# A graph layer and a mixture of experts: token groups of 7 x 512, 256, 128 and 128, and a first expert octet beside the list

## The chip, the cores and the metric

The kernel runs on one core of a Trainium2 chip. The metric is the device time of one execution in microseconds; the time before is the median of three runs, 401.93 us (399.69 to 402.66).

## What is computed

Two layers, each added to its input. The first mixes the rows of all 4096 tokens by a dense 4096 x 4096 adjacency matrix; the second sends each token to two of 64 experts.

```python
def _L0_gnn_ref(x, adj, kernel, bias, beta):
    scale = jnp.reciprocal(jnp.sum(adj, axis=1) + beta)
    agg = adj @ x + beta[:, None] * x
    return scale[:, None] * agg @ kernel + bias

def _L0_ffn_ref(x, Wr, br, W1, b1, W2, b2):
    ...
    logits = xf @ Wr + br
    topk_logits, topk_idx = jax.lax.top_k(logits, TOP_K)       # TOP_K = 2
    gates = jax.nn.softmax(topk_logits, axis=1)
    ...
    for e in range(E):                                          # E = 64
        h = jax.nn.relu(xf @ W1[e] + b1[e])                     # 128 -> 256
        y = h @ W2[e] + b2[e]                                   # 256 -> 128
        out = out + combine[:, e:e + 1] * y
...
x = x + _L0_gnn_ref(_layernorm(x, axis=-1), adj, ...)
x = x + _L0_ffn_ref(_layernorm(x, axis=-1)[None], ...)[0]
```

## The kernel before

Work on each engine is written out by hand, in the order in which that engine runs it; semaphores tie the engines together. TensorE is PE in the profile, VectorE DVE, ScalarE ACT, GpSimd POOL, SyncE SP.

**Aggregation.** The 4096 tokens are 32 tiles of 128, taken in eight groups of four (512 tokens). For a group g, the adjacency columns come in eight chunks of 1 MB through a ring of five slots (`adj_ring`, loaded on SP's queue). A chunk holds four tiles of 128 source tokens by 512 columns. TensorE adds up z^T x chunk in the PSUM bank `agg_ps[g % 2]`. Most chunks are split into a high and a low part: ScalarE rounds the chunk (`round_chunk`, line 584), VectorE subtracts (`low_part`, line 716), and TensorE runs three fast products for each tile (lines 973, 974, 977). The others are whole chunks (`whole_chunk`, line 963): one 32-bit product a tile. Seven chunks of each group from the second on are split (51 in all), and the last, which holds the group's own rows, is whole, since VectorE first adds beta on its diagonal (`add_diag`).

**The steps of a group.** While TensorE aggregates group g, the steps of group g - 1 run between its products at fixed tile numbers (`step`): `copy_agg` (ACT), `gnn` (PE, the weight product and the degree), `residual` with statistics (DVE), `root` (ACT), `shifts` (DVE), `normalise` (ACT, writes z1), `turn_z1` (PE), `copy_z1t` (ACT), `router` (PE), `choose` (DVE, the two experts of each token), `ranks` (PE, each token's place among its expert's), `place` (DVE), and `dispatch` (POOL), which scatters each token's row to its expert's rows in memory, eight indirect DMAs a group. For the last group these steps stand alone.

**Two lists of expert tiles.** An expert tile is 128 rows of one expert. The early list is made from the first seven groups: 16 full tiles, whose starts are known while the last group is still under way. The list of the remaining tiles needs all tokens: `total_done`, 26 small VectorE steps (lines 823 to 853), a transposition on TensorE, and the two tables `table` and `skip_tab`. TensorE runs 13 and 12 products of no effect (`warm`, line 918) around that transposition.

**Expert tiles.** Eight slots. Each tile needs its weights and rows (loaded on SP's queue for slots 0 to 3, on ACT's for 4 to 7), then `turn_x` (PE, line 1039), `copy_xt` (DVE, 874), `up` (PE, 1045), `relu` (DVE, 884), `down` (PE, 1052 and 1055), `copy_y` (ACT, 645) and an indirect scatter of the answers (POOL, 542). `ahead` runs the three PE steps and the two DVE steps with distances of up to three tiles. The number of tiles in groups of four, `quads`, is read from `table` into a register by every engine. SP and ACT load the tiles of the next octet as slots come free. At the end both answers of a token are read back and summed with the gates.

## Time and profile before

| | |
|---|---|
| median of the runs | 401.93 us (399.69 to 402.66) |
| the profiled execution's own time | 402.74 us |
| its span | 400.9 us |
| TensorE busy | 345.6 us, 86% |
| VectorE busy | 306.9 us, 77% |
| ScalarE busy | 171.0 us, 43% |
| GpSimd busy | 224.7 us, 56% |
| mean granted clock of TensorE | 0.941 of full speed |

The span is the time from the first to the last instruction in the trace; the profiled execution took 1.84 us more. Busy time is that of the instructions themselves, an average over stages with different limits. A row of the timeline gives start and duration in us, engine, line of the program, operation, what it writes and reads, how many instructions are merged, and in brackets the idle time before and what ended it. For TensorE one row can hold several records; a 32-bit product makes two.

### The profile page before, as it was taken

How to read it: one execution, taken by the hardware profiler on the slowest of the kernel's cores; microseconds unless marked ns; L12 is line 12 of the kernel's file. 1: busy time of each engine (PE TensorE's matmuls, PEld its weight loads, DVE VectorE, ACT ScalarE, POOL GpSimd, SP SyncE). 2: the span in 40 equal slices, each digit the busy share in tenths (PEclk: the TensorE clock that was granted, in tenths of full speed). 3: DMA queues.
4: the chain of work that ended last, by engine and by line, in shares of the span. 5: the costliest groups of instructions: out<-in, count | busy, mean ns of one | idle time of the engine just before them, and what ended most of it. 6: DMA issues, size and time to landing. Idle time of an engine off the chain costs nothing.

```text
span 400.9 us, 8275 instructions
## 1 busy us (share of the span) xinstructions
PE 345.6 (86%) x1975; PEld 276.7 (69%) x1975; DVE 306.9 (77%) x907; ACT 171.0 (43%) x265; POOL 224.7 (56%) x220
## 2 busy tenths in 40 slices
PE   5999898997999999999999835999999999999100
PEld 2445684884886868868778522799999999999000
DVE  3769779779889899898998568676777776777067
ACT  2475665556665855748646031111222212122063
POOL 4450002038877847768578354657777777777500
PEclk9799999998999999999999966999999999999855
DMA  8999999995996978969965017499999999995097
GB/s 308 361 428 366 345 425 367 370 428 241 381 425 251 417 319 329 411 244 412 385 263 216 13 41 256 124 317 285 308 293 291 296 292 289 293 291 163 25 372 257
DMA packets 45624, 119.26 MB, mean 298 GB/s; under 512 B 7705, under 2 KB 19630, under 8 KB 37410
## 3 DMA queue, kind: packets, MB, share of 16 engines
q1 hardware_dynamic: 27938, 95.88, 63.7%
q10 hardware_dynamic: 12672, 14.58, 11.9%
q0 software_dynamic: 4992, 8.54, 5.8%
q8 instruction: 9, 0.15, 0.1%
q14 instruction: 13, 0.11, 0.1%
HBM read 104.02 MB, written 16.78 MB: 301 GB/s over the span
## 4 chain that ended last, share of the span: by engine, by line
PE 39%; DVE 33%; DMA 14%; ACT 7%; issue 4%; POOL 1%; SPq 0%; POOLq 0%; DVEq 0%; ACTq 0%
DVE adj_low L716 16%; DMA adj_ring<-adj_t 9%; PE bank L1045 9%; PE bank L963 8%; PE bank L1055 5%; PE bank_pair L1055 5%; ACT adj_high L584 4%; ACT payload L599 2%; PE bank L1039 2%; PE bank_pair L1052 2%; PE bank L1052 2%; DVE x_sb L905 2%; DVE adj_ring L745 2%; DVE top_i L755 2%; DMA expert_answers<-adj_ring,ans 2%
## 5 line engine op out<-in xcount | busy, mean ns | idle before, releaser
L716 DVE TENSOR_TENSOR adj_low<-adj_ring,adj_high 128x2048 fp32r<-128x2048 f32 x51 | 116.1, 2286 | 19.7 <-ACT adj_high L584 19.3
L584 ACT CAST adj_high<-adj_ring 128x2048 fp32r<-128x2048 f32 x51 | 97.1, 1905 | 60.0 <-DMA adj_ring<-adj_t 36.2
L529 POOL DMA_INDIRECT dispatched_rows<-payload,slot x64 | 94.4, 1475 | 46.2 <-DMA dispatched_rows<-pad_rows 19.3
L542 POOL DMA_INDIRECT expert_answers<-adj_ring,ans x92 | 90.4, 983 | 31.9 <-issue 18.6
L973 PE MATMUL bank<-adj_high,z_hi 128*128 128x512 f32 x204 | 84.4, 414 | 0.0
L974 PE MATMUL bank<-adj_high,z_lo 128*128 128x512 f32 x204 | 79.7, 391 | 0.0
L884 DVE TENSOR_SCALAR adj_ring<-bank,adj_ring 128x128 f32<-128x128 f32 x184 | 56.1, 346 | 8.8 <-PE bank L1045 6.2
L1045 PE MATMUL bank<-xt_sb,adj_ring 128*128 128x128 f32 x368 | 56.2, 275 | 0.3 <-DVE xt_sb L874 0.3
L977 PE MATMUL bank<-adj_low,z_hi 128*128 128x512 f32 x204 | 54.8, 390 | 0.9 <-DVE adj_low L716 0.9
L963 PE MATMUL bank<-adj_ring,z_sb 128*128 128x512 f32 x104 | 51.3, 645 | 3.1 <-DVE z_sb L702 3.1
L1045 PEld LDWEIGHTS bank<-xt_sb,adj_ring 128*128 128x128 f32 x368 | 48.4, 192 | 0.5 <-DVE xt_sb L874 0.5
L518 POOL TENSOR_TENSOR more<-mask 128x128 bf16<-128x128 bf16 x8 | 12.9, 1618 | 59.2 <-DVE mask L761 59.1
L977 PEld LDWEIGHTS bank<-adj_low,z_hi 128*128 128x128 f32 x204 | 38.2, 188 | 9.6 <-DVE adj_low L716 1.3
L973 PEld LDWEIGHTS bank<-adj_high,z_hi 128*128 128x128 f32 x204 | 38.4, 188 | 9.0 <-issue 1.8
L974 PEld LDWEIGHTS bank<-adj_high,z_lo 128*128 128x128 f32 x204 | 38.4, 188 | 8.8 <-issue 1.7
L963 PEld LDWEIGHTS bank<-adj_ring,z_sb 128*128 128x128 f32 x104 | 20.9, 208 | 27.0 <-issue 25.7
L645 ACT COPY adj_ring<-bank_pair 128x128 f32<-128x128 f32 x46 | 11.3, 267 | 63.5 <-PE bank_pair L1055 58.3
L879 DVE TENSOR_TENSOR ans<-adj_ring,skip_tab 128x1 int32<-128x1 f32 x92 | 14.9, 162 | 22.5 <-DMA expert_answers<-adj_ring,ans 20.4
L1055 PE MATMUL bank_pair<-adj_ring 128*128 128x128 f32 x184 | 28.7, 278 | 0.1
L1055 PE MATMUL bank<-adj_ring 128*128 128x128 f32 x184 | 28.6, 278 | 0.1
L645 ACT COPY adj_ring<-bank 128x128 f32<-128x128 f32 x46 | 12.1, 267 | 37.7 <-PE bank L1055 34.7
L874 DVE COPY xt_sb<-bank 128x128 f32<-128x128 f32 x92 | 25.7, 281 | 1.8 <-PE bank L1039 1.8
(151 smaller groups left out, 424.6 us busy)
## 6 DMA issues: line engine op xcount, KB each, us to landing
adj_ring<-adj_t SPq DMA_DIRECT2D x64, 1024.0 KB, 9.2
adj_ring<-w_pack SPq DMA_DIRECT2D x48, 257.5 KB
adj_ring<-w_pack ACTq DMA_DIRECT2D x44, 257.5 KB
dispatched_rows<-pad_rows SPq DMA_DIRECT2D x8, 528.0 KB, 12.0
adj_ring<-expert_answers SPq DMA_DIRECT2D x8, 512.0 KB, 6.6
adj_ring<-dispatched_rows SPq DMA_DIRECT2D x48, 66.0 KB
adj_ring<-dispatched_rows ACTq DMA_DIRECT2D x44, 66.0 KB
out<-x_sb SPq DMA_DIRECT2D x8, 256.0 KB, 4.2
```

Of the source, the lines that this page charges most:

```text
L529: pool.indirect_dma_start(rows, bass.IndirectOffsetOnAxis(ap=slot[:, b, t, k:k + 1], axis=0), payload[:, b, t, k, :], None).then_inc(scatt ...
L542: pool.indirect_dma_start(y_tok, bass.IndirectOffsetOnAxis(ap=ans[:, s:s + 1], axis=0), y_sb[:, s, :], None, bounds_check=N * K - 1, oob_i ...
L584: nc.scalar.copy(high[:, m % PARTS], adj_sb[:, slot_of(g, k)]).then_inc(hi_ready, 1)
L716: v.tensor_tensor(low[:, m % PARTS], adj_sb[:, slot_of(g, k)], high[:, m % PARTS].bitcast(F32), ALU.subtract).then_inc(lo_ready, 1)
L874: v.tensor_copy(xt_sb[:, s % 2, :], xt_ps[s % 2][:, 0:P]).then_inc(xt_ready, 1)
L884: last = v.tensor_scalar(h_sb[:, s % DEEP, c, :], up_ps[s % 2][:, c * P:(c + 1) * P], w_sb[:, s, B1_COL + c:B1_COL + c + 1], 0.0, ALU.add, ...
L963: last = mm(agg_ps[g % 2][:], z_sb[:, j, :], adj_sb[:, slot_of(g, k), u, :], start=(k + u == 0), stop=(k + 1 == CHUNKS and u + 1 == CJ))
L973: mm(agg_ps[g % 2][:], z_hi[:, first + u, :], high[:, m % PARTS, u, :], start=(k + u == 0), stop=False)
L974: mm(agg_ps[g % 2][:], z_lo[:, first + u, :], high[:, m % PARTS, u, :], start=False, stop=False)
L977: last = mm(agg_ps[g % 2][:], z_hi[:, first + u, :], low[:, m % PARTS, u, :], start=False, stop=False)
L1045: last = mm(up_ps[s % 2][:, c * P:(c + 1) * P], w_sb[:, s, c * P:(c + 1) * P], xt_sb[:, s % 2, :], start=True, stop=True)
L1055: last = mm(y, h_sb[:, s % DEEP, c, :], w_sb[:, s, H + c * D:H + (c + 1) * D], start=False, stop=(c == HC - 1))
```

## The change

It cuts the last 512 tokens into groups of 256, 128 and 128. `TILES_OF` gives the tiles of each group, `FULL` (7) is the group of 256. A chunk stays 1 MB: it holds eight source tiles of 256 columns, or sixteen of 128, so the groups have 4, 2 and 2 chunks. Of these only three chunks of the group of 256 are split. The steps of the small groups stand at tile numbers of their own. The early list is still made from the first seven groups, now during the group of 128 that comes next. All eight early loads are on SP's queue, and they wait until the chunks but the last two are used. The first eight expert tiles are written out ahead of the loop and no longer wait for the list; VectorE's steps for the list stand between them, in five parts. The warming products around the list are gone. The ring starts one slot further on, and a few PSUM banks are used otherwise (`last_ps` is the logits' bank, so the fourth tile's answer goes to the first bank).

```diff
-GROUPS = N // GN
+TILES_OF = (4, 4, 4, 4, 4, 4, 4, 2, 1, 1)
+GROUPS = len(TILES_OF)
+FIRST_TILE = tuple(sum(TILES_OF[:g]) for g in range(GROUPS))
+FULL = TILES_OF.index(2)
...
-SPLIT = 7
 FIRST_SPLITS = (5, 6)
+SPLITS = tuple((g, k) for g in range(GROUPS)
+               for k in (FIRST_SPLITS if g == 0 else range(7) if g < FULL else range(3) if g == FULL else ()))
...
+        def ahead_once(turn, s, steps):
+            for distance, step in steps:
+                n = s + distance
+                step(turn + n // SLOTS, n % SLOTS)
...
             sp.wait_ge(early_table_ready, 1)
-            starts = load_starts(SP, early_table, 0, SP_SLOTS)
-            for s in range(SP_SLOTS):
+            starts = load_starts(SP, early_table, 0, SLOTS)
+            sp.wait_ge(chunk_used, chunk_no(GROUPS - 1, 0))
+            for s in range(SLOTS):
                 load_weights(sp, starts[s], s)
-            wait_scattered_before_last(sp)
-            for s in range(SP_SLOTS):
+            wait_full_scattered(sp)
+            for s in range(SLOTS):
                 load_rows(sp, starts[s], s)
...
+            for g in range(FULL, GROUPS):
+                if g == GROUPS - 2:
+                    act.wait_ge(early_list_turned, 1)
+                    nc.scalar.copy(early_table[:], early_ps[0:1, E:E + EARLY]).then_inc(early_table_ready, 1)
+                copy_agg(g)
+                root(g)
+                normalise(g)
+                copy_z1t(g)
...
+            residual(FULL)
+            shifts(FULL)
+            add_diag(FULL + 1)
+            list_early()
+            choose(FULL)
+            for g in range(FULL + 1, GROUPS):
+                residual(g)
+                if g + 1 < GROUPS:
+                    add_diag(g + 1)
+                    place(g - 1)
+                    shifts(g)
+                else:
+                    shifts(g)
+                    place(g - 1)
+                choose(g)
             place(GROUPS - 1)
...
-            for half in range(2):
-                ahead(dve, 0, half, None, steps)
+            for s in range(SLOTS):
+                ahead_once(0, s, steps)
+                if s == 0:
+                    list_counts()
+                if s == 1:
+                    list_totals()
+                if s == 2:
+                    list_experts()
+                if s == 3:
+                    list_starts()
+                if s == 5:
+                    list_to_tables()
+                if s == 6:
+                    make_gates()
+            dve.wait_ge(skip_ready, 1)
+            dve.wait_ge(table_ready, 1)
+            quads = quads_in_use(dve)
...
+            def step_last(j):
+                if j == 2:
+                    gnn(FULL + 1)
+                if j == 5:
+                    ranks(FULL)
+                if j == 14:
+                    turn_z1(FULL + 1)
+                if j == 17:
+                    router(FULL + 1)
+                if j == 24:
+                    ranks(FULL + 1)
...
-            warm(13, turn_ps)
-            pe.wait_ge(list_ready, 1)
-            nc.tensor.transpose(last_ps[0:2, 0:P], lst[:], ident[:])
...
-            warm(12, turn_ps)
...
+            pe.wait_ge(seen_ready, GROUPS)
+            mm(last_ps[:, 0:E], ones_b[:], seen[:], start=True, stop=True).then_inc(total_done, 1)
+            steps = [(3, turn_x), (0, down), (2, up)]
+            for s in range(SLOTS):
+                if s == SLOTS - 1:
+                    pe.wait_ge(skip_ready, 1)
+                ahead_once(0, s, steps)
+                if s == 4:
+                    pe.wait_ge(list_ready, 1)
+                    nc.tensor.transpose(last_ps[0:2, 0:P], lst[:], ident[:])
+                    mm(last_ps[:, P:2 * P], ones_f[:], again_diag[:], start=True, stop=True).then_inc(list_turned, 1)
+            pe.wait_ge(table_ready, 1)
+            quads = quads_in_use(pe)
+            with pe.Fori(1, OCTETS) as turn:
```

TensorE's queue from the end of the aggregation to the first expert tile, before (L963 is the aggregation, L930 `gnn`, L1039 `turn_x`):

```order
L963 MATMUL bank<-adj_ring,z_sb 128x512 x4
L1013 MATMUL bank<-seen,ones_b 128x64 [waits seen_ready]
L930 MATMUL bank_pair<-gnn_w_and_degree,agg_sb 128x129 [waits agg_copied,wd_ready,var1]
L930 MATMUL bank_pair<-gnn_w_and_degree,agg_sb 128x129 x3
L936 MATMUL bank<-ident,payload 128x128 [waits z1_ready]
...
L1022 MATMUL bank_pair<-seen,ones_b 128x64 [waits seen_ready]
L918 MATMUL bank<-ones_b 128x512 x13
L1025 MATMUL bank_pair<-ident,lst 2x128 [waits list_ready]
L1026 MATMUL bank_pair<-again_diag,ones_f 128x128
L918 MATMUL bank<-ones_b 128x512 x12
L333 TENSOR_LOAD table [waits table_ready,skip_ready]
L333 ISA x2
L1039 MATMUL bank<-ident,adj_ring 128x128 [waits xt_ready,tile_in0]
```

The same place after (L1064 is the aggregation, L1027 `gnn`, L1033 `turn_z1`, L1039 `router`, L1048 and L1049 `ranks`, L1180 `turn_x`):

```order
L1064 MATMUL bank<-adj_ring,z_sb 128x128 x8
L1027 MATMUL bank_pair<-gnn_w_and_degree,agg_sb 128x129 [waits agg_copied,wd_ready,var1]
L1033 MATMUL bank<-ident,payload 128x128 [waits z1_ready]
L1039 MATMUL bank<-wr_sb,z1t 128x64 [waits z1t_ready]
L1048 MATMUL bank<-mask,before 128x64 [waits seen_ready,mask_ready]
L1049 MATMUL bank<-seen,ones_b 128x64
L1180 MATMUL bank<-ident,adj_ring 128x128 [waits xt_ready,tile_in0]
L1180 MATMUL bank<-ident,adj_ring 128x128 [waits xt_ready,tile_in1]
L1186 MATMUL bank<-xt_sb,adj_ring 128x128 [waits h_ready,xt_ready]
```

The list's products and the warming ones have left this place, and each step has one tile in place of four. The same engine within the last group of 128, after (L1051 is the end of `ranks` of the group of 256):

```order
L1027 MATMUL bank_pair<-gnn_w_and_degree,agg_sb 128x129 [waits agg_copied,wd_ready,var1]
L1064 MATMUL bank<-adj_ring,z_sb 128x128 x3
L1048 MATMUL bank<-mask,before 128x128 [waits seen_ready,mask_ready]
L1049 MATMUL bank<-seen,ones_b 128x128
L1051 MATMUL bank<-mask,ones_b 128x64
L1064 MATMUL bank<-adj_ring,z_sb 128x128 x9
L1033 MATMUL bank<-ident,payload 128x128 [waits z1_ready]
L1064 MATMUL bank<-adj_ring,z_sb 128x128 x2
L1064 MATMUL bank<-adj_ring,z_sb 128x128 [waits diag_added,adj_in4]
L1039 MATMUL bank<-wr_sb,z1t 128x64 [waits z1t_ready]
L1064 MATMUL bank<-adj_ring,z_sb 128x128 x7
```

Steps that had 32 tiles of 512 columns around them stand between tiles of 128 here. VectorE's queue at the first expert tiles, before (L853 and L856 end the list, L874 is `copy_xt`, L879 and L884 `relu`):

```order
L853 TENSOR_SCALAR again_diag<-ident,again 128x128 [waits dve_own]
L856 CAST table<-bank_pair 2x128 [waits dve_own,list_turned]
L858 TENSOR_SCALAR skip_tab<-bank_pair,iota_back 128x128
...
L333 TENSOR_LOAD table [waits dve_own,skip_ready]
L333 ISA x2
L874 COPY xt_sb<-bank 128x128 [waits up_done,x_turned] x2
L879 TENSOR_TENSOR ans<-adj_ring,skip_tab 128x1
L884 TENSOR_SCALAR adj_ring<-bank,adj_ring 128x128 [waits down_done,up_done]
L884 TENSOR_SCALAR adj_ring<-bank,adj_ring 128x128
L874 COPY xt_sb<-bank 128x128 [waits up_done,x_turned]
```

And after (L896 follows the last `place`, L956 `copy_xt`, L961 and L966 `relu`, L900 the list's first step):

```order
L896 TENSOR_TENSOR diff<-top 128x32
L956 COPY xt_sb<-bank 128x128 [waits up_done,x_turned] x2
L961 TENSOR_TENSOR ans<-adj_ring,skip_tab 128x1
L966 TENSOR_SCALAR adj_ring<-bank,adj_ring 128x128 [waits down_done,up_done]
L966 TENSOR_SCALAR adj_ring<-bank,adj_ring 128x128
L956 COPY xt_sb<-bank 128x128 [waits up_done,x_turned]
L961 TENSOR_TENSOR ans<-adj_ring,skip_tab 128x1
L966 TENSOR_SCALAR adj_ring<-bank,adj_ring 128x128 [waits down_done,up_done]
L966 TENSOR_SCALAR adj_ring<-bank,adj_ring 128x128
L956 COPY xt_sb<-bank 128x128 [waits up_done,x_turned]
L900 TENSOR_SCALAR spare<-bank 128x64 [waits total_done]
```

The whole list has moved from ahead of the first `copy_xt` to behind the fourth, and its parts stand behind one tile each.

## Rows read from the trace of the kernel before

**Rows 1.** Stretches: PE, PEld, DVE, ACT, POOL busy (instructions), then PEclk, DMA share, GB/s.
```profile
202.50:228.40 25.90, 25.57 (x118) 19.40 (x117) 21.13 (x44) 10.78 (x12) 17.10 (x13) 1.00 0.46 184
228.40:253.70 25.30, 12.80 (x56) 7.24 (x57) 16.23 (x84) 5.21 (x10) 13.87 (x17) 0.73 0.42 140
270.70:378.60 107.90, 100.32 (x869) 98.22 (x869) 73.33 (x313) 20.39 (x80) 82.52 (x84) 0.99 0.86 262
```

**Rows 2.** Timeline of GpSimd: the ninth and the last of 92 answer scatters.
```profile
270.71 0.98 POOL L542 DMA_INDIRECT expert_answers<-adj_ring,ans  x1 [3.07 <-ACT adj_ring L645]
...
377.54 0.98 POOL L542 DMA_INDIRECT expert_answers<-adj_ring,ans  x1 [0.31 <-issue]
```

**Rows 3.** Timeline of ScalarE: the eighth tile's copy to the ninth's.
```profile
265.07 0.27 ACT L645 COPY adj_ring<-bank 128x128 f32<-128x128 f32 x1 [0.96 <-PE bank L1055]
...
265.75 1.21 ACTq L351 DMA_DIRECT2D adj_ring<-dispatched_rows  x1
269.58 0.43 ACT L645 COPY adj_ring<-bank_pair 128x128 f32<-128x128 f32 x2 [4.25 <-PE bank L1055]
```

**Rows 4.** Timeline of TensorE: chunks, the tail's transposition and router, the first tile.
```profile
94.10 5.20 PE L963 MATMUL bank<-adj_ring,z_sb 128*128 128x512 f32 x8
...
198.80 3.68 PE L963 MATMUL bank<-adj_ring,z_sb 128*128 128x512 f32 x8
...
206.06 0.40 PE L973 MATMUL bank<-adj_high,z_hi 128*128 128x512 f32 x1
...
208.79 0.39 PE L973 MATMUL bank<-adj_high,z_hi 128*128 128x512 f32 x1
...
224.68 3.68 PE L963 MATMUL bank<-adj_ring,z_sb 128*128 128x512 f32 x8
...
235.86 1.12 PE L936 MATMUL bank<-ident,payload 128*128 128x128 f32 x4 [5.60 <-ACT payload L599]
237.65 1.97 PE L942 MATMUL bank<-wr_sb,z1t 128*128 128x64 f32 x8 [0.68 <-ACT z1t L606]
...
253.67 0.38 PE L1039 MATMUL bank<-ident,adj_ring 128*128 128x128 f32 x2
```

**Rows 5.** Timeline of VectorE: two low parts, then the tail's residual and choice.
```profile
201.86 4.49 DVE L716 TENSOR_TENSOR adj_low<-adj_ring,adj_high 128x2048 fp32r<-128x2048 f32 x2
...
230.29 0.18 DVE L721 RECIPROCAL scale<-bank_pair 128x4 f32<-128x4 f32 x1 [3.74 <-PE bank_pair L930]
...
239.66 0.42 DVE L750 TENSOR_TENSOR logits<-bank,br_sb 128x256 f32<-128x256 f32 x1 [2.80 <-PE bank L942]
...
242.40 0.42 DVE L761 TENSOR_TENSOR mask<-hot 128x256 bf16<-128x256 f32 x1
```

**Rows 6.** Timeline of VectorE: first and last of 26 steps of the list.
```profile
245.56 0.22 DVE L823 TENSOR_SCALAR spare<-bank_pair 128x64 f32<-128x64 f32 x1
...
250.35 0.29 DVE L853 TENSOR_SCALAR again_diag<-ident,again 128x128 f32<-128x128 f32 x1
```

**Rows 7.** Timeline of VectorE: the ReLU of the first tile and of the second.
```profile
255.07 0.61 DVE L884 TENSOR_SCALAR adj_ring<-bank,adj_ring 128x128 f32<-128x128 f32 x2 [0.54 <-PE bank L1045]
...
255.86 0.60 DVE L884 TENSOR_SCALAR adj_ring<-bank,adj_ring 128x128 f32<-128x128 f32 x2
```

**Rows 8.** TensorE in the expert tiles: timeline, and the group of the weight loads.
```profile
256.29 0.61 PE L1045 MATMUL bank<-xt_sb,adj_ring 128*128 128x128 f32 x4
256.73 0.27 PE L1039 MATMUL bank<-ident,adj_ring 128*128 128x128 f32 x1
...
257.51 0.61 PE L1045 MATMUL bank<-xt_sb,adj_ring 128*128 128x128 f32 x4
...
L1045 PEld LDWEIGHTS bank<-xt_sb,adj_ring 128*128 128x128 f32 x368 | 48.4, 192 | 0.5 <-DVE xt_sb L874 0.5
```

**Rows 9.** Timeline of SyncE's queue: four early weight loads.
```profile
241.87 2.01 SPq L348 DMA_DIRECT2D adj_ring<-w_pack  x4
```

**Rows 10.** A stretch of the tail, columns as in rows 1.
```profile
234.00:247.00 13.00, 6.92 (x26) 4.14 (x27) 8.52 (x43) 3.41 (x7) 4.58 (x8) 0.50 0.36 123
```

More of the change, by code:

```diff
@@ L47 @@
 BUFS, DEEP = 2, 4
+LIST_BANK = 3
 EARLY = 2 * SLOTS
@@ L749, in choose @@
                 dve.wait_ge(logits_done, g + 1)
-                own.after(v.tensor_tensor(logits[:], logit_ps, br_sb[:, None, :].to_broadcast([P, GT, E]), ALU.add))
-                for t in range(GT):
-                    last = v.max(top[:, g * GT + t, :], logits[:, t, :])
+                span, count = span_of(g), TILES_OF[g]
+                own.after(v.tensor_tensor(logits[:, span], logit_ps[:, span], br_sb[:, None, :].to_broadcast([P, count, E]), ALU.add))
+                for n, t in enumerate(tiles_of(g), FIRST_TILE[g]):
+                    last = v.max(top[:, n, :], logits[:, t, :])
@@ new lines, in list_experts @@
+            def list_experts():
+                v.tensor_reduce(first, lw[:], AX_X, ALU.max)
+                v.scalar_tensor_tensor(out=own_handled[:], in0=iota_e[:], scalar=expert, in1=handled[:], op0=ALU.is_equal, op1=ALU.mult)
+                own.after(v.scalar_tensor_tensor(out=own_spare[:], in0=iota_e[:], scalar=expert, in1=spare[:], op0=ALU.is_equal, op1=ALU.mult))
+                v.tensor_reduce(latest, own_spare[:], AX_X, ALU.add)
+                own.after(v.tensor_reduce(held, own_handled[:], AX_X, ALU.add))
@@ L1005, in step @@
-                    if j == 20:
-                        router(g - 1)
-                    if j == 28:
-                        ranks(g - 1)
-                for k in range(CHUNKS):
+                    if g < FULL:
+                        step_full(g, j)
+                    elif g == FULL:
+                        step_half(j)
+                    elif g == FULL + 1:
+                        step_next(j)
+                    else:
+                        step_last(j)
+                for k in range(chunks_of(g)):
```

458 lines of the change are left out of this document (257 added, 201 removed).

## Prediction

> **What bounds the kernel now.** Read by stages, the span falls into a first part that is alike in both kernels up to about 202 us, the last group of 512 tokens (202.5 to 228.4), a tail (228.4 to 253.7), the expert tiles (to 378.6) and the final sum. Up to 228.4 VectorE sets the pace with the splits of the adjacency chunks: 21.1 of 25.9 us [rows 1]. In the tail nothing is full: TensorE works 12.8 of 25.3 us at a mean clock of 0.73, and one chain of small steps goes from engine to engine. The expert stage looks as if TensorE bounded it (100.3 of 107.9 us). GpSimd's own rows say otherwise [rows 2]: from the answer that starts at 270.71 to the last at 377.54 there are 83 steps of 1.287 us, without one break. So from the ninth tile on GpSimd's answer scatters are the bound, and **the end of the span is the start of the ninth scatter plus a constant**: 83 x 1.287 us and a last part that the change doesn't touch. What the change is worth is read at 270.71. That scatter waited 3.07 us for ScalarE's copy of 269.58 [rows 2, 3], and the copy was late because ScalarE, after the eighth tile's copy (265.07), issues loads and reads the list into registers: 4.5 us from one to the other.
>
> So the sum has four terms, each between marks of its own: (a) the end of the last aggregation product, now 228.4; (b) from there to the first transposition of an expert tile, now 253.67 [rows 4]; (c) from there to the eighth answer's copy, now 11.4 us later; (d) from there to the ninth scatter, 5.6 us.
>
> **(a) The last 512 tokens as groups of 256, 128 and 128: later by 10.0 us.** Four chunks fewer are split (47 in place of 51); that frees VectorE and ScalarE, but neither bounds this stretch any more. What bounds it is TensorE's order with three dependent chains in it.
>
> Group of 256: a split chunk's 12 products of 512 columns take 2.73 us (206.06 to 208.79) [rows 4], so 0.114 for one of 256 columns; I take 0.12. After the preceding whole chunk (198.80 with 3.68, so to 202.1 in steady order) 56 of them and 1.3 us for the preceding group's weight product bring TensorE to 210.2. There it waits for z1 of that group. VectorE ends its last low part at 206.35 and begins the residual; from the residual to the transposition of z1 takes 5.57 us in the tail (230.29 to 235.86) [rows 4, 5], where no split stands between, so 211.85. This wait of 1.6 us is new. Transposition, copy and router follow: 1.12 and 1.97 us in the rows, which were at half clock (0.50 from 234 to 247) [rows 10], so 0.6, 0.6 and 1.0, to 214.1. Ten more split products and six tiles of the whole chunk (8 records in 3.68 us for 512 columns, so 0.44 a tile) go to 218.1. The choice (239.66 to 242.82, 3.16 us) [rows 5] is there at 217.3, so the ranks don't wait. They and two tiles end the group at 219.4.
>
> Each group of 128 has 32 tiles of 128 columns. Their price stands in the expert stage, with 32-bit products of that very shape: 4 records from 256.29 to 256.73, 0.111 each [rows 8], two a tile, 7.1 us for 32. The first group has inside it the preceding one's steps (1.55 us), the early list's transposition (0.3) and 0.1 of waiting: 9.0 us, to 228.4. The second has 1.5 us of steps and waits about 0.75 for its z1, since the first one's residual, statistics and normalising (some 3.5 us) are longer than the tiles put before it: 9.35 us, to 237.8. With 0.6 for hand-overs that I don't see, 238.4. From both sides: no wait and no missed hand-over gives 236.5, a fall of the clock after the long wait and a late chain 241. I take 238.4, the sum of the rows.
>
> **(b) From the last product to the first tile: 25.3 us become 7.6.** What goes is three quarters of each step, the list of the remaining tiles (245.56 to 250.64 on VectorE, 5.1 us) [rows 6] with its transposition, and the warming products ahead of the tiles. What stays is a chain for one tile, estimated from the same steps for four: copy 0.27, product 0.4, residual and statistics 1.1, root 0.3, reciprocal and shift 0.35, normalising 0.6, transposition 0.3, copy 0.3, router 0.4, choice 1.25, ranks 0.3, place and difference 1.1: 6.7, and 0.9 for some fifteen hand-overs. The signal that lets TensorE begin a tile stands on VectorE behind that last place. The first tile starts at 238.4 + 7.6 = 246.0. Ends: 7.0 without hand-overs, 9.2 if the steps shrink less than that.
>
> Costed at nothing, with their cover: SyncE now issues all eight early loads, at 0.5 us an issue [rows 9]. The table is ready at about 228.4, some 2 us go for registers and 8 for sixteen issues, so the last is out at 238.5, 7 us ahead; without this cover the late tiles would cost their delay. ScalarE's wait for the early table stands ahead of the first small group's copy, but the transposition it waits for is ahead of that group's last product in TensorE's queue. GpSimd scatters the last two groups by about 249; behind them stand all answers, and the first is there at 251, so 2 us are the cover.
>
> **(c) The first eight tiles: 11.4 us become 15.6.** The list's steps now stand between the tiles on VectorE. A tile alone takes 0.79 us there (255.07 to 255.86) [rows 7], against 1.22 on TensorE (256.29 to 257.51) [rows 8]: the slack of eight tiles is 3.4 us. Into it go 5.1 us of list and 0.5 for the two steps of the tables, each like the list's last (0.29). VectorE therefore runs without a break: way in 2.2 us (253.67 to 255.86), six tiles 4.7, list 5.6, a ReLU 0.5, the last product 0.7, which is 13.7. To it comes the clock. At 94.10 a whole chunk took 5.20 us in place of 3.68 [rows 4]: half clock for twice the difference, 3 us, under steady products. Nothing warms TensorE between 238.4 and 246 in the changed kernel, so I let the first tiles run 3 us at half clock: 1.0 on the way in and 0.9 in the first tile. That makes 15.6 us, 261.6 for the eighth copy. Ends: 12.5 (list in the slack, clock up), 22 (all eight at half clock). TensorE's two new waits, for the list after the fifth tile and for the skip table before the eighth, have all later products queued behind them; VectorE is the late one there in any case, and its delay is already counted.
>
> **(d) The hand-over to the ninth tile: unchanged**, 5.6 us: ScalarE's instructions are the same and the table is ready by then. A row issue of 1.21 us [rows 3] may shrink to the usual third of it: 0 to -0.9. The ninth scatter then starts at 267.2 against 270.71.
>
> **Sum.** +10.0 - 17.7 + 4.2 + 0 = **-3.5 us**. On the profiled execution's 402.74 us that is 399.2; the runs' median, 401.93, is 0.8 lower, so **398.4 us**, 0.9% faster. 1% (4 us) is about what a measurement of this kernel can tell from no change.
>
> **A rule that speaks against it.** The 128-column records of the expert stage follow each other at 0.111 us, though the weight loads beside them last 0.192 us each [rows 8]: the loads overlap. The Trainium skill, TensorE: Matmul & The Clock Gate, section "LDWEIGHTS (loading the stationary operand)", gives a load the time of its columns, 107 ns for 128, and its section on weight-path modes says that the fast load isn't for FP32. Were such a load paid beside every record of the small groups, an estimate from that page is 128 x 0.107 = 13.7 us more. The rows of the expert stage don't agree with that.
>
> **Rivals.** *Loads not hidden (slower).* The products of the small groups go at the pace of their weight loads: 128 records x (0.192 - 0.111) = 10.4 us, and 72 split products of 256 columns x 0.07 = 5.0, so +15.4 - 3.5, or 413.8 us. It decides from a pitch of 0.14 us (no gain) and 0.17 (1% slower). For it: narrow products need a load four times as often. Against it: the 368 records of that shape in the expert stage. Chance 0.06.
>
> *The clock.* Each fall costs what it cost at 94.10, 1.5 us. The changed tail has two waits that could bring one (1.6 and 0.75 us), and the eight tiles may stay at half clock for longer. Two falls give 401.4 us, no change; with all eight tiles at half clock 404 to 407. For it: the warming products are gone. Against it: the two waits are shorter than the stretch from the tail's last step (231) to its fall. Chance 0.16, half of it slower by over 1%.
>
> *The list is hidden after all.* If VectorE's steps fit beside the tiles, (c) is 12.4 and the sum -6.7: 395.2 us. For it: the last tiles have slack again. Against it: 5.6 us don't go into 3.4. Chance 0.12.
>
> **How the numbers follow.** The forecast has 0.66, with a range of its own of 395 to 401.5 from the ends of (a) and (b); two fifths of that lie beyond 1% faster. So faster 0.27 + 0.12 and a little for an easier boundary, 0.41; slower 0.06 + 0.08, 0.14; within 1% 0.45. The range for 8 in 10 is 394.5 to 403.5: it takes in the hidden list and two falls of the clock, and leaves out the paid loads and eight tiles at half clock.
>
> **What would show it.** In the new profile the last 128-column aggregation product should end near 238, and records of that shape should follow at 0.11 us. The first tile's transposition should stand near 246, the eighth copy near 261.6, the ninth scatter near 267, and from there steps of 1.287 us with no break to the last; the span should be near 397.4. VectorE should have nearly no idle time in the first five tiles. I am wrong if GpSimd has breaks after the ninth answer, if the last aggregation product ends beyond 241, or if the clock is still half after 250.

## The result and the profile after

The changed kernel takes **396.46 us** (median of 18 runs, 393.78 to 399.89) against 400.49 us for the kernel before (18 runs, 399.03 to 402.66). The ratio is 0.9886, 95% interval 0.9865 to 0.9907: 1.1% faster, or 4.6 us with an interval of 3.7 to 5.4. The forecast was 3.5 us, 398.4 us from the 401.93 us of the first three runs (397.0 from the 400.49 of all 18), and "within 1%". The profiled execution took 396.82 us, its span is 395.0 us and its mean granted clock 0.954.

Read first by stages. The marks are those of the prediction's four terms: the start of the seventh group's last whole chunk and ScalarE's copy of the last aggregation product, then the first tile's transposition and the eighth copy, and last the end of the scatters. Columns as in [rows 1].

```profile
198.93:234.40 35.47, 33.33 (x265) 31.25 (x263) 23.04 (x92) 7.26 (x17) 23.90 (x28) 1.00 0.53 191
234.40:241.65 7.25, 1.51 (x8) 0.89 (x8) 4.11 (x21) 1.43 (x4) 2.36 (x4) 0.83 0.66 220
241.65:257.25 15.60, 14.49 (x101) 13.18 (x102) 13.10 (x69) 3.38 (x9) 7.92 (x9) 0.86 0.54 158
257.25:373.10 115.85, 105.48 (x917) 103.22 (x915) 77.43 (x334) 21.85 (x85) 84.47 (x86) 0.98 0.85 257
```

The tail of 25.3 us is 7.25 us long, the stage ahead of it is longer, and VectorE is busy for 13.10 of the 15.60 us of the first eight tiles. TensorE's timeline (start, duration, line, idle time before and what ended it) answers to [rows 4 and 8].

```profile
195.81 3.68 PE L1064 MATMUL bank<-adj_ring,z_sb 128*128 128x512 f32 x8
...
208.84 0.66 PE L1033 MATMUL bank<-ident,payload 128*128 128x128 f32 x4 [1.22 <-ACT payload L655]
...
218.00 3.38 PE L1064 MATMUL bank<-adj_ring,z_sb 128*128 128x128 f32 x28
...
229.60 0.33 PE L1033 MATMUL bank<-ident,payload 128*128 128x128 f32 x1 [0.60 <-ACT payload L655]
...
232.34 2.03 PE L1064 MATMUL bank<-adj_ring,z_sb 128*128 128x128 f32 x16
237.82 0.33 PE L1033 MATMUL bank<-ident,payload 128*128 128x128 f32 x1 [2.54 <-ACT payload L655]
...
241.65 0.66 PE L1180 MATMUL bank<-ident,adj_ring 128*128 128x128 f32 x2 [0.92 <-DVEq L950]
...
266.08 0.33 PE L1180 MATMUL bank<-ident,adj_ring 128*128 128x128 f32 x1 [0.25 <-DMA adj_ring<-dispatched_rows]
...
267.91 0.33 PE L1180 MATMUL bank<-ident,adj_ring 128*128 128x128 f32 x1 [0.39 <-DMA adj_ring<-dispatched_rows]
...
271.61 0.32 PE L1180 MATMUL bank<-ident,adj_ring 128*128 128x128 f32 x1 [2.26 <-DMA adj_ring<-dispatched_rows]
```

Three things are to be seen. The chunk that starts at 198.80 in [rows 4] starts at 195.81 here, though nothing ahead of it was to change. The two forecast waits for z1 are there (1.22 and 0.60 us). And three transpositions wait for rows from memory. TensorE transposes three tiles ahead of the one that it finishes, so these are the 18th to the 20th tile, the second to the fourth that SyncE loads for the third octet. (The expectations below call them tiles 14 to 16, by a miscount of mine.) ScalarE's timeline from the eighth copy to the ninth answers to [rows 3], GpSimd's (the ninth, the 17th, the 25th and the last answer) to [rows 2].

```profile
257.25 0.27 ACT L698 COPY adj_ring<-bank 128x128 f32<-128x128 f32 x1 [0.96 <-PE bank L1200]
...
257.93 0.34 ACTq L387 DMA_DIRECT2D adj_ring<-dispatched_rows  x1
260.59 0.43 ACT L698 COPY adj_ring<-bank_pair 128x128 f32<-128x128 f32 x2 [3.08 <-PE bank_pair L1200]
```
```profile
261.71 0.98 POOL L588 DMA_INDIRECT expert_answers<-adj_ring,ans  x1 [2.24 <-ACT adj_ring L698]
...
273.84 0.98 POOL L588 DMA_INDIRECT expert_answers<-adj_ring,ans  x1 [2.13 <-ACT adj_ring L698]
...
285.62 0.98 POOL L588 DMA_INDIRECT expert_answers<-adj_ring,ans  x1 [1.79 <-ACT adj_ring L698]
...
371.90 0.98 POOL L588 DMA_INDIRECT expert_answers<-adj_ring,ans  x1 [0.30 <-issue]
```

GpSimd now has two breaks behind the ninth answer, where the prediction had none. From ninth to last it takes 110.19 us in place of 106.83: 3.36 us are given back.

Because the profiled executions differ ahead of any change, each term is counted from the start W of that last whole chunk of the seventh group (198.80 before, 195.81 after). A second profile of the changed kernel was taken (W at 199.68).

| us | before | forecast | after | after, again |
|---|---|---|---|---|
| (a) W to the copy of the last aggregation product | 29.60 | 39.6 | 38.60 | 38.61 |
| (b) to the first tile's transposition | 25.27 | 7.6 | 7.24 | 7.25 |
| (c) to the eighth copy | 11.40 | 15.6 | 15.60 | 15.70 |
| (d) to the ninth scatter | 5.64 | 5.6 | 4.46 | 4.51 |
| W to the ninth scatter | 71.91 | 68.4 | 65.90 | 66.07 |
| ninth to last scatter | 106.83 | 106.83 | 110.19 | 107.34 |

### The profile page after: what moved, and what is told of

Its sections match the earlier page's. It is cut to its first block, busy times and chain, and to the rows that moved or that the text cites. A ratio compares the mean times of both kernels' runs of the same rounds, so it can differ in the third digit from the quotient of the medians.

```text
span 395.0 us, 8459 instructions
## 1 busy us (share of the span) xinstructions
PE 341.3 (86%) x2076; PEld 282.6 (72%) x2076; DVE 301.6 (76%) x923; ACT 166.0 (42%) x267; POOL 220.9 (56%) x221
## 4 chain that ended last, share of the span: by engine, by line
PE 44%; DVE 29%; DMA 14%; ACT 8%; issue 3%; SPq 1%; POOLq 0%; DVEq 0%; POOL 0%; ACTq 0%
DVE adj_low L769 14%; PE bank L1064 10%; PE bank L1186 10%; DMA adj_ring<-adj_t 8%; PE bank_pair L1200 5%; PE bank L1200 5%; ACT adj_high L640 4%; ACT payload L655 3%; PE bank L1180 3%; PE bank_pair L1197 3%; PE bank L1197 2%; PE bank L1082 2%; DVE x_sb L1002 2%; DMA expert_answers<-adj_ring,ans 2%; DMA x_sb<-x 2%
## 5 line engine op out<-in xcount | busy, mean ns | idle before, releaser
L769 DVE TENSOR_TENSOR adj_low<-adj_ring,adj_high 128x2048 fp32r<-128x2048 f32 x47 | 106.9, 2286 | 15.7 <-ACT adj_high L640 15.2
L580 POOL DMA_INDIRECT dispatched_rows<-payload,slot x64 | 91.5, 1430 | 48.0 <-DMA dispatched_rows<-pad_rows 17.9
L640 ACT CAST adj_high<-adj_ring 128x2048 fp32r<-128x2048 f32 x47 | 89.5, 1906 | 53.8 <-DMA adj_ring<-adj_t 32.7
L1078 PE MATMUL bank<-adj_high,z_hi 128*128 128x512 f32 (+1 forms) x200 | 79.5, 401 | 0.7 <-ACT adj_high L640 0.7
L1079 PE MATMUL bank<-adj_high,z_lo 128*128 128x512 f32 (+1 forms) x200 | 74.7, 378 | 0.0
L1064 PE MATMUL bank<-adj_ring,z_sb 128*128 128x128 f32 (+2 forms) x240 | 64.7, 421 | 4.3 <-DVE z_sb L755 4.3
L966 DVE TENSOR_SCALAR adj_ring<-bank,adj_ring 128x128 f32<-128x128 f32 x184 | 56.0, 345 | 12.8 <-PE bank L1186 10.5
L1064 PEld LDWEIGHTS bank<-adj_ring,z_sb 128*128 128x128 f32 x240 | 36.5, 194 | 25.4 <-issue 23.5
L1082 PE MATMUL bank<-adj_low,z_hi 128*128 128x512 f32 (+1 forms) x200 | 50.7, 378 | 0.2 <-DVE adj_low L769 0.2
L1082 PEld LDWEIGHTS bank<-adj_low,z_hi 128*128 128x128 f32 x200 | 36.1, 188 | 7.7 <-DVE adj_low L769 0.6
L1180 PE MATMUL bank<-ident,adj_ring 128*128 128x128 f32 x92 | 25.9, 284 | 4.1 <-DMA adj_ring<-dispatched_rows 2.9
L961 DVE TENSOR_TENSOR ans<-adj_ring,skip_tab 128x1 int32<-128x1 f32 x92 | 14.8, 160 | 17.9 <-DMA expert_answers<-adj_ring,ans 13.9
## 6 DMA issues: line engine op xcount, KB each, us to landing
dispatched_rows<-pad_rows SPq DMA_DIRECT2D x8, 528.0 KB, 11.4
```

The costliest lines, as they stand in the source:

```text
L580: pool.indirect_dma_start(rows, bass.IndirectOffsetOnAxis(ap=slot[:, b, t, k:k + 1], axis=0), payload[:, b, t, k, :], None).then_inc(scatt ...
L640: nc.scalar.copy(high[:, m % PARTS], adj_sb[:, slot_of(g, k)]).then_inc(hi_ready, 1)
L769: v.tensor_tensor(low[:, m % PARTS], adj_sb[:, slot_of(g, k)], high[:, m % PARTS].bitcast(F32), ALU.subtract).then_inc(lo_ready, 1)
L966: last = v.tensor_scalar(h_sb[:, s % DEEP, c, :], up_ps[s % 2][:, c * P:(c + 1) * P], w_sb[:, s, B1_COL + c:B1_COL + c + 1], 0.0, ALU.add, ...
L1064: last = mm(agg_ps[g % 2][:, 0:TILES_OF[g] * P], z_sb[:, j, :], chunk[:, u, :], start=(k + u == 0), stop=(k + 1 == chunks_of(g) and u + 1 ...
L1078: mm(agg, z_hi[:, first + u, :], high_part[:, u, :], start=(k + u == 0), stop=False)
```

## The experiments

Two theories. **Theory 1** is the prediction's: the end is the ninth scatter plus a constant, and its four terms were only mis-sized. **Theory 2**: behind the ninth scatter a new wait takes the bound's place, and the early start is paid for there.

**The part ahead of the change.** First the changed kernel once more.

> The changed kernel itself, for a second profile: it tells which of the readings of the first are chance. The last whole chunk of the seventh group can stand anywhere from 195.8 to 199.0; the four terms of the chain should repeat within 0.3 us. The waits for the rows of tiles 14 to 16 (0.25, 0.39, 2.26 us) and the breaks before the 17th and 25th scatter (2.13, 1.79) repeat if they belong to the change, and shrink towards 0.7 us each, as with the warming products, if the late loads of that execution were chance.

It took 398.07 us. Each of the four terms repeats within 0.10 us, their sum within 0.17. The three waits for rows don't: TensorE has none, the break before the 17th scatter shrinks to 0.80 and that before the 25th is gone. GpSimd's timeline in that profile (ninth, 16th, 17th):

```profile
265.75 0.98 POOL L588 DMA_INDIRECT expert_answers<-adj_ring,ans  x1 [2.29 <-ACT adj_ring L698]
...
274.76 0.98 POOL L588 DMA_INDIRECT expert_answers<-adj_ring,ans  x1 [0.31 <-issue]
276.53 0.98 POOL L588 DMA_INDIRECT expert_answers<-adj_ring,ans  x1 [0.80 <-ACT adj_ring L698]
```

So most of the 3.36 us belonged to one execution. The break of 0.80 us that is left has no late load in it: there ScalarE's copy of the 17th tile comes 3.53 us after that of the 16th (271.87 and 275.40). Then the ring alone:

```diff
-    return chunk_no(g, k) % RING
+    return (chunk_no(g, k) + 1) % RING
```


> The kernel before with the ring of adjacency chunks started one slot further on, as the change does; nothing else. In the two profiles the changed kernel is 3.0 us ahead at the last whole chunk of the seventh group (195.81 against 198.80) although the order of work is the same up to there. If the shift of the ring makes that, this kernel gains about 3 us against before (397.5) and its profile has that chunk near 196. If it is chance in the first 100 us, where transfers set the pace, the time is that of before within 1 us.

400.71 us, 0.9989 of before (0.9961 to 1.0017): nothing. Its W is 196.44 with the work of the kernel before:

```profile
196.44 3.68 PE L963 MATMUL bank<-adj_ring,z_sb 128*128 128x512 f32 x8
```

Over all fourteen profiles W lies between 195.5 and 199.7, the changed kernel's own two at 195.81 and 199.68, so the 3.0 us by which the two first profiles differ at W are chance of the first 200 us, and only differences counted from W are the change's.

**The two halves alone.** The small groups, with the list ahead of the first tile (TensorE's total and list transposition move likewise):

```diff
             steps = [(1, relu), (3, copy_xt)]
+            list_counts()
+            list_totals()
+            list_experts()
+            list_starts()
+            list_to_tables()
             copy_xt(0, 0)
```


> The small groups stay, the list of the remaining tiles is computed ahead of the first tile. Theory 1 (the prediction's chain: the end is the ninth answer scatter plus a constant): the list's 5.1 us and its transposition go before the tiles, eight tiles run at TensorE's pace, so the eighth copy moves from 257.25 to about 261.4 and the end by as much, +4.1 us against the changed kernel (about 400.6). Theory 2 (from the ninth scatter on the loads of the second and third octet are late, and 3.4 us of breaks on GpSimd are the price of an early start): the eighth copy moves the same, but the two breaks of 2.13 and 1.79 us shrink to the usual 0.30, so the end moves by +0.7 (about 397.2). Which it is, is read from GpSimd's breaks after the ninth answer.

400.31 us, 0.9979 of before (0.9952 to 1.0006), and so some 3.7 us slower than the changed kernel by the ratios. The ninth scatter stands at W + 69.99, 3.9 to 4.1 us later than with the list beside the tiles, as both theories had it. Behind it there is one break of 1.00 us, and the last scatter stands at W + 177.54: 1.45 us behind the first profile of the changed kernel, 4.13 behind the second. The timings side with theory 1, and so does the second profile.

Then the other half, eight groups of 512 with the list beside the tiles and without the warming products:

```diff
-TILES_OF = (4, 4, 4, 4, 4, 4, 4, 2, 1, 1)
+TILES_OF = (4, 4, 4, 4, 4, 4, 4, 4)
...
+            total_early()
             gnn(GROUPS - 1)
             turn_z1(GROUPS - 1)
             router(GROUPS - 1)
+            turn_early_list()
             ranks(GROUPS - 1)
```


> The other half of the change alone: eight groups of 512 as before, but the list of the remaining tiles computed beside the first eight tiles, without the warming products. The early table comes late, as before (about 239.9 in its profile), so the first tile must wait for its loads (issued to 246.1, landing some 2 us later): first transposition near 247.5 in place of 253.67, eighth copy 15.6 us later at 263.1 in place of 265.07, ninth scatter 4.5 us behind: 267.6 in place of 270.71, so -3.1 us, of which the octet boundaries give back 0.5 to 1: about 398.4. If the two halves only work together (the loads not being there), no gain: 400.5.

402.60 us, 1.0040 of before (1.0014 to 1.0067): slower, which neither number had. TensorE's timeline, and ScalarE's with the first and the eighth copy:

```profile
249.74 0.47 PE L1185 MATMUL bank<-ident,adj_ring 128*128 128x128 f32 x1 [7.40 <-DMA adj_ring<-dispatched_rows]
```
```profile
254.53 0.27 ACT L702 COPY adj_ring<-bank_pair 128x128 f32<-128x128 f32 x1 [7.98 <-PE bank_pair L1205]
...
265.79 0.27 ACT L702 COPY adj_ring<-bank 128x128 f32<-128x128 f32 x1 [0.96 <-PE bank L1205]
```

TensorE stands 7.40 us for the first tile's rows, so the first transposition gains only 2.47 us on before (W + 52.40 against 54.87), while (c) is 16.05, 4.65 longer, and the ninth scatter stands at W + 72.92, 1.0 us later than before. The change as a whole gains 4.6 us where its halves give 0.8 faster (in an interval that reaches no change) and 1.6 slower. Here the early table is written at 238.41 and the loads go out from 240.41; in the changed kernel they go out from 228.03 and the last is out 4.3 us ahead of the first tile. So the small groups bring the loads forward, and the list beside the tiles gains only where they are there:

```profile
228.03 4.39 SPq L384 DMA_DIRECT2D adj_ring<-w_pack  x8
232.67 4.63 SPq L387 DMA_DIRECT2D adj_ring<-dispatched_rows  x8
```

**The clock.** 22 products of no effect in TensorE's waits of the last group:

```diff
             gnn(GROUPS - 1)
+            warm(8, agg_ps[GROUPS % 2])
             turn_z1(GROUPS - 1)
+            warm(2, agg_ps[GROUPS % 2])
             router(GROUPS - 1)
+            warm(6, agg_ps[GROUPS % 2])
             ranks(GROUPS - 1)
+            warm(6, agg_ps[GROUPS % 2])
```


> The changed kernel with 22 products of no effect in TensorE's waits of the last group's steps. If the clock sets the way from the first transposition to the first answer's copy (4.67 us at half clock, 2.82 us in the kernel before at full clock), the first copy comes 1.85 us earlier and the end -1.9 us (about 394.6), since both the answers and the next loads hang on it. Rival: VectorE sets it (the list's first part stands there), or the products themselves delay the steps of the last group; then the first copy stays within 0.5 us or comes later, and the end is unchanged or up to 1 us later.

395.12 us, 0.9852 of before (0.9813 to 0.9890). The clock by stretches, of the changed kernel and then of this one (columns as above; the third from the end is PEclk, times full speed), and this kernel's first and eighth copy:

```profile
239.00:240.00 1.00, 0.00 (x0) 0.00 (x0) 0.90 (x5) 0.00 (x0) 0.70 (x1) 0.62 0.00 0
240.00:246.00 6.00, 4.47 (x21) 3.88 (x22) 3.87 (x20) 1.51 (x2) 3.24 (x4) 0.50 0.13 45
246.00:247.00 1.00, 1.00 (x10) 1.00 (x10) 0.90 (x5) 0.27 (x1) 0.00 (x0) 0.96 0.07 16
```
```profile
236.00:247.00 11.00, 9.25 (x58) 5.63 (x57) 6.76 (x34) 3.20 (x7) 4.49 (x6) 1.00 0.48 158
```
```profile
246.39 0.27 ACT L698 COPY adj_ring<-bank_pair 128x128 f32<-128x128 f32 x1 [1.32 <-PE bank_pair L1204]
```
```profile
258.10 0.27 ACT L698 COPY adj_ring<-bank 128x128 f32<-128x128 f32 x1 [0.96 <-PE bank L1204]
```

At full clock the way from the first transposition (243.57) to the first copy (246.39) takes 2.82 us in place of 4.67: 1.85 less, near the 1.9 that the prediction had let the half clock cost. But the eighth copy gains only 0.9 (W + 60.52 against 61.44): once the clock is up, VectorE with its list is late (ScalarE's waits ahead of the fifth and the sixth copy, 1.55 and 2.43 us, are the same in both profiles). The half clock is worth 1 us here by the marks, not 1.9. By the medians it is 1.3 us, and the intervals of the two ratios overlap.

**What stands behind the ninth answer.** Take bytes away:

```diff
+            if light:
+                eng.dma_start(w_sb[0:1, s], w_pack[bass.ds(start // EXPERT_ROWS, 1), 0, :]).then_inc(tile_in[s], 16)
+            else:
+                load_weights(eng, start, s)
             load_rows(eng, start, s)
```


> The changed kernel, with the weights of tiles 8 to 15 left out of their loads (one partition of 128 is moved), so their answers are of wrong weights; it takes 2.1 MB out of the transfers between 246 and 262 us. Theory 2 (late loads make the breaks): TensorE's waits for the rows of tiles 14, 15 and 16 (0.25, 0.39 and 2.26 us) vanish, the break before the 17th scatter shrinks from 2.13 to 0.30 us, and that before the 25th too if it only follows from the first; the end -1.8 to -3.4 us (393.1 to 394.7). Rival (ScalarE's reads of the list into registers, some 3.2 us at every octet, make the breaks): both breaks stay, the end is unchanged.

396.25 us, 0.9854 of before (0.9806 to 0.9902, four runs). The breaks are 0.71 and 0.61 us, one wait for rows (0.86 us, the 20th tile) is left. Against the first profile that is theory 2's gain; against the second, which has breaks of 0.80 and 0.30 with all bytes moved, it is none. The runs show 1.3 us less than the changed kernel by the ratios and 0.2 by the medians, and the intervals overlap. It does not settle it. Next ScalarE's reads of tile starts, which stand in one piece behind the eighth copy of an octet:

```diff
-                    starts = load_starts(ACTIVATION, table, turn * SLOTS + (SLOTS + SP_SLOTS - EARLY), SLOTS - SP_SLOTS)
+                    starts = []
                     for s in range(SLOTS):
                         copy_y(turn, s)
-                        if s >= SP_SLOTS:
+                        if s < SP_SLOTS:
+                            starts += load_starts(ACTIVATION, table, turn * SLOTS + (SLOTS + SP_SLOTS + s - EARLY), 1)
+                        else:
                             load_tile(act, starts[s - SP_SLOTS], s)
```


> The changed kernel, with ScalarE's read of four tile starts into registers, which stands in one piece behind the eighth copy of every octet, taken apart: one start behind each of the first four copies, where ScalarE idles 0.96 us a tile. Theory 2a (the breaks after the ninth answer come from ScalarE's 3.2 us between the eighth copy of an octet and the next, which show now that TensorE is only one or two tiles ahead): the gap shrinks to some 1.2 us, the ninth scatter comes 0.5 to 1.5 us earlier, and the breaks before the 17th and 25th scatter fall to 0.30 where no load is late: -1.5 to -3 us against the changed kernel. Theory 2b (late loads alone make the breaks): they stay as they are, the end changes by less than 0.5 us.

395.54 us, 0.9862 of before (0.9835 to 0.9889). ScalarE's gap from the eighth copy to the next falls from 3.34 to 1.99 us and (d) from 4.5 to 3.17; one break of 0.93 us stays before the 17th scatter, that before the 25th is gone. The ninth scatter is 1.3 to 1.5 us earlier, the last 1.3 earlier than in the second profile of the changed kernel. The runs show 0.9 us of it by the medians, and the intervals overlap.

The same edit in the kernel before:

> The kernel before, with only ScalarE's reads of tile starts taken apart. It tests the premise that the end is the ninth scatter plus a constant: from the eighth copy to the ninth scatter it takes 5.6 us now, of which some 1.5 us of reading goes; the row issue of 1.21 us may stay. GpSimd then runs without a break from a ninth scatter 1.5 us earlier: 399.0 in place of 400.5. If the loads set the end there too, a break before the 13th or 17th scatter takes it back and the time is that of before.

399.34 us, 0.9968 of before (0.9935 to 1.0002). The ninth scatter is at W + 70.39 against 71.91, the last at W + 177.47 against 178.74: the end follows the ninth scatter, less 0.25 us, which is a break of 0.53 us ahead of the 25th. The time agrees with that, though its interval just reaches 1.

Both edits of the changed kernel together:

> The reads taken apart and the 22 products of no effect together. If both act on different places (the way in, and the octet's end), the gains add: that of the warming products (1.3 us by the runs) and that of the reads (1.5 to 3 us by theory 2a, none by 2b): 392 to 394 us by 2a, 395 by 2b.

395.34 us, 0.9842 of before (0.9801 to 0.9883): not shown to be better than either (0.9862 and 0.9852). Here theory 2 has its place. The ninth scatter comes at W + 63.70, 2.3 us earlier, and then TensorE waits 1.69 us for the rows of the 20th tile, and GpSimd has breaks of 1.88 and 0.43 us.

**Loads of the second octet in buffers of their own.** They go out right behind the first eight tiles', when the transfers stand nearly still (45 GB/s from 240 to 246, above):

```diff
-            starts = load_starts(SP, early_table, SLOTS, SP_SLOTS)
-            for s in range(SP_SLOTS):
-                next_tile(starts[s], 0, s)
+            starts = load_starts(SP, early_table, SLOTS, SLOTS)
+            sp.wait_ge(chunk_used, chunk_no(GROUPS - 1, 1) + 1)
+            for s in range(SLOTS):
+                sp.dma_start(w_of(1, s), w_pack[bass.ds(starts[s] // EXPERT_ROWS, 1)].rearrange("a p c -> (a p) c")).then_inc(next_in[s], 16)
+                sp.dma_start(xin_next[:, s], rows[bass.ds(starts[s], P), :]).then_inc(next_in[s], 16)
```


> The changed kernel, with the weights and rows of tiles 8 to 15 loaded into buffers of their own (the room of the aggregation's left operands and the free end of the ring) right behind those of tiles 0 to 7, from about 238 us on, when the transfers are nearly idle (41 GB/s from 240 to 245 us), and not as the first tiles are done; the second octet is written out as the first is. If late loads are what costs the changed kernel its waits for the rows of tiles 14 to 16 and the breaks behind the ninth answer, these waits vanish, in every execution, and the time falls by the mean of what two profiles show (3.3 and 0.5 us): some 1.9 us against the changed kernel, 394.5, with less spread. If ScalarE's gap at the octet's end makes the breaks, one of some 0.5 us stays and the time is 396.

396.08 us, 0.9878 of before (0.9847 to 0.9910): no gain, a miss. SyncE's loads for the third octet are in time, but now one of ScalarE's row issues holds it for 1.51 us (266.57), 2.03 us stand ahead of its copy of the 16th tile in place of 0.96, its reads follow, and the break before the 17th scatter is 1.78 us. The rows of that issue are late as well: TensorE waits 0.89 us for them (272.22). With the other two edits:

> Own buffers for the second octet, the reads taken apart and the warming products. Without late loads the earlier ninth scatter of the kernel with reads apart and warming products (63.7 us behind the seventh group's last whole chunk, in place of 65.9 to 66.1) is kept to the end: -2.3 us, and no break: -0.5 to -3.3. Against the changed kernel -2.8 to -5, so 391.5 to 393.7. If the loads are late again at the third octet, where they wait for slots as before, 1 to 1.5 us of that are lost.

**393.11 us, 0.9798 of before (0.9769 to 0.9828)**: better than both kernels. Its six runs lie within 1.2 us (392.75 to 393.92). GpSimd's timeline, the ninth and the last answer:

```profile
260.94 0.98 POOL L605 DMA_INDIRECT expert_answers<-adj_ring,ans  x1 [0.95 <-ACT adj_ring L715]
...
367.80 0.98 POOL L605 DMA_INDIRECT expert_answers<-adj_ring,ans  x1 [0.30 <-issue]
```

From ninth to last it is 106.86 us, without a break, as before the change (106.83). And without the warming products:

> Own buffers for the second octet and the reads taken apart, without the warming products. With all three the time was 393.11 us. In the two profiles with warming products the eighth copy stands 60.5 us behind the seventh group's last whole chunk, without them 61.4 to 61.6. If that 1 us is the clock's whole price, and the two others already remove GpSimd's breaks, this kernel takes 394.1 with no break over 0.3 us behind the ninth answer. If the warming products are needed for more (they shift the loads as well), breaks come back and it takes 395 or more; if they are worth nothing by now, 393.1.

394.52 us, 0.9837 of before (0.9787 to 0.9887); from ninth (262.21) to last (369.10) 106.89 us without a break. In this profile, the only one of it, the two edits that keep ScalarE and the loads out of the way suffice for the constant. The clock is worth more than the 1 us expected: the eighth copy stands at W + 62.17 against 60.53 with the warming products, and the medians differ by 1.4 us, though the intervals overlap. The granted clock is 0.50 from 239 to 248 us here, from 240 to 246 in the changed kernel's first profile.

## Where the prediction was wrong, and where it was right

The chain was right: every mark that it names is there. Two steps failed. The first is the size of two terms of the sum: (a) was put at +10.0 us and measured +9.0, and (d) was put at 0, though its own ends were 0 to -0.9, and measured -1.15. With them went the forecast of 0.9%, "within 1%": up to the ninth scatter the gain is 5.8 to 6.0 us in place of 3.5. The second is the premise that the end is the ninth scatter plus a constant: in the changed kernel 0.5 and 3.4 us are given back behind the ninth answer, which the sum put at nothing.

- **(a), the last 512 tokens, "later by 10.0 us"**: it is 9.0. The walk itself held: TensorE is released by z1 at W + 13.03 (forecast 13.05), and the two waits are 1.22 and 0.60 us (1.6 and 0.75); the granted clock stays at 1.00 through both. What failed is the addition of 0.6 us "for hand-overs that I don't see", of which the trace shows nothing. The rest is 0.25 us in the first group of 128 (8.75 in place of 9.0: its first product starts at 216.28, the next group's at 225.04) and 0.13 in the group of 256. 28 records of 128 columns take 3.38 us, 0.12 each, a quarter of the 0.46 of a record of 512 columns (8 in 3.68 us). The rival of loads that aren't hidden is false: the weight loads beside them last 194 ns each (the page's group for the line) and yet lie under the products.

```profile
L1064 PEld LDWEIGHTS bank<-adj_ring,z_sb 128*128 128x128 f32 x240 | 36.5, 194 | 25.4 <-issue 23.5
```

  The Trainium skill (TensorE: Matmul & The Clock Gate, "LDWEIGHTS (loading the stationary operand)") gives a load of 128 columns 107 ns by its formula; the trace has 194. Nor does the trace agree with the prediction's estimate from it, 13.7 us more if a load were paid beside every record: the first group of 128 took 8.75 us, less than the 9.0 forecast without such a price.
- **(b), 25.3 to 7.6 us**: 7.24.
- **(c), 11.4 to 15.6 us**: 15.60 and 15.70, but that the sum is met is luck: two errors cancel. VectorE is busy 13.10 us of it. The half clock lasts until 246, 4.4 us into the tiles where I had let 3, and taking it away gives back 1 us, not 1.9, since VectorE is late in any case. At full clock, with the warming products, (c) is 14.53, where the walk without the clock had 13.7. Against the 11.40 before, that is 3.1 us for the list, which is not hidden.
- **(d), "unchanged, 5.6 us"**: 4.46 and 4.51. ScalarE's fourth row issue takes 0.34 us in place of 1.21, and 0.3 us more went. I had given 0 to -0.9 as its ends and taken 0. In the profile with the ring moved that issue took 2.09 us and (d) 6.22 us: in all three profiles of the old order ScalarE is held for longest (1.42 us with the reads taken apart), in both of the changed kernel SyncE alone, where it doesn't delay the ninth copy. Why ScalarE is spared there is not shown, so this term is as uncertain as the hold itself.
- **Ninth to last, "a constant"**: it holds for the kernel before (106.83) and nearly for the second profile after (107.34), not for the first (110.19). I had named it as what would show me wrong. In [rows 3] ScalarE is so late at the ninth copy that four tiles are ready and are copied from 269.58 to 270.35 (first line below, right behind the last of [rows 3]). In the changed kernel two are ready there. That TensorE's lead had covered what came late is argued from this; no run changes the lead alone. Two things reach GpSimd with the smaller lead: ScalarE's 3.3 us at the octet's end, and loads that go out late. SyncE's queue in the first profile, the row issues of the 18th, 19th and 20th tile, stands second:

```profile
269.90 0.45 ACT L645 COPY adj_ring<-bank 128x128 f32<-128x128 f32 x2
```
```profile
261.23 1.10 SPq L387 DMA_DIRECT2D adj_ring<-dispatched_rows  x1
...
263.15 2.08 SPq L387 DMA_DIRECT2D adj_ring<-dispatched_rows  x1
...
266.04 0.33 SPq L387 DMA_DIRECT2D adj_ring<-dispatched_rows  x1
```

  Two of them hold SyncE for 1.10 and 2.08 us in place of 0.33. The fourth tile's room was free at 264.2 (the copy of its predecessor), its loads go out from 265.52, and TensorE waits for them until 271.61. In the second profile the held issues of that octet are 0.86 and 0.94 us, and nobody waits. It looks like the 1.21 us of [rows 3] on the other queue. Why an issue is held, and for how long, stays open: taking bytes away didn't settle it, nor did own buffers alone. Shown is only that its cost goes when ScalarE's gap is taken apart and the second octet is loaded early: the kernel with all three edits has held issues of 0.86 and 1.18 us on SyncE behind the first octet, and no break, in one profile.

From W to the ninth scatter the sum is -6.0 and -5.8 us against the forecast's -3.5: 1.0 from (a), 0.3 from (b), 1.15 from (d). Of that 0.5 us is given back in one profile and 3.4 in the other. The runs' 4.6 us lie between (5.3 and 2.7). The kernel before varies too: against the profile with the ring moved, whose last scatter stands at W + 179.41, the two would be 6.0 and 3.3. The prediction's own range, 395 to 401.5 us, doesn't follow from the ends of (a) and (b) that it names: they give 395.9 to 402.6. *The list is hidden after all* gave 395.2 us, near the measured time, but by luck: its (c) of 12.4 is false.

## What to carry to other kernels

A chain of marks, each term from rows, gave the gain to within 2.5 us of 6, and its two largest errors were choices, not rows: a reserve of 0.6 us for waits that no row shows, and the term (d), taken at one end of its own range. Keep a reserve in the range, not in the sum. "The start of the bound stage plus a constant" is only as good as the lead that the engines ahead of it have at that point: when a change starts the stage earlier, count how many pieces were ready ahead and what they covered. Two halves of a change can be worth nothing or less alone when one of them makes the other's inputs ready; and marks of two profiles are compared from the last point at which both still do the same work.

## What the runs showed of the hardware

- The first 200 us, alike in all kernels, end anywhere within 4.2 us (W from 195.5 to 199.7); the steps behind W repeat within 0.2 us up to the ninth answer in the changed kernel's two profiles.
- A single issue of a 66 KB load holds its engine for up to 2.1 us in place of 0.33, now on SyncE (2.08 us at 263.15, changed kernel), now on ScalarE (2.09 at 263.39, ring moved), with the transfers 0.73 and 0.95 busy meanwhile; 1.19 us were held at 247.03 with 0.37. Rows issued at 266.04 were there only at 271.6. The Trainium skill (DMA: Bandwidth & Descriptors, "Issuing engines are not separate DMA queues") says that DMAs run on the same 16 engines whichever engine issued them, and that fits loads that are late on either queue.
- Between ScalarE's last issue of an octet and its next copy pass some 2.3 us (257.93 + 0.34 to 260.59), in which it reads four tile starts into registers and starts the loop's next turn. Read one by one between copies, the same reads leave 1.99 us from the eighth copy to the ninth in place of 3.34.
